# A language-model tower on one core: two biases moved from TensorE to VectorE, two buffers of transposed rows, a loop of two turns, small products ahead of the last z

## The chip, the cores and the metric

The kernel runs on one core of a Trainium2 chip. The metric is the device time of one execution in microseconds (us). The median of three runs of the kernel before is 1307.63 us (1302.93 to 1309.92). A change of this kernel under about 0.5%, 6.5 us, can't be told from none.

## What is computed

64 sequences of 128 token ids go through four stages. All is fp32 unless said.

```python
table = concat([quantize_ste(tw[i] * ts[i], [16, 8, 6, 4][i]) for i in range(4)])   # 50257 x 256
x = layernorm(take(table, ids))
# block: Mamba-like mixer, then an MLP
proj = rms(x) @ in_proj_w.T                 # z (512), u (512), B, C (16 each), dt (8 heads)
u, B, C = silu(causal depthwise conv of 4 taps + conv_b); B, C normalised; dt = softplus(dt + dt_bias)
# two-state recurrence over 128 steps for 8 heads x 64 x 16, read out with C -> ys
x = x + ((ys + D_skip * u) * silu(z)) @ out_proj_w.T + out_proj_b
x = x + gelu(rms(x) @ fc1_w.T + fc1_b) @ fc2_w.T + fc2_b
# layernorm, one absmax over everything, int8 rounding, int8-weight product, scale, bias, add x
```

The quantising of the table needs the largest magnitude of each tier, so the whole table of 51 MB is read once.

## The kernel before

**Stage 1** (0 to 175 us, lines 163 to 415). SyncE streams the table into a ring of six tiles. ScalarE takes magnitudes (L248), VectorE folds them into running maxima (L346), GpSimd gathers the token rows (L232), TensorE makes each token's tier scale (L286), and VectorE multiplies it into pairs of tokens (L337, `scale_tokens`). In the same stream VectorE scales `w_in` by the first norm's weights (L390), unpacks `w_q` (L391) and makes `ident_b` (L393). The late weights are loaded last (`LATE_WEIGHTS`, L222). A barrier ends the stage.

**Stage 2** (175 to 1250 us). 16 groups of four sequences (512 tokens) go through a software pipeline of 19 turns, written once per engine (`pe_turn`, `act_turn`, `dve_turn`, `pool_turn`) and called by `turns`. In turn g group g is in its first part (norm, transposes, u, small products B, C, dt), group p = g-1 in its second (z, scan, output product) and group m = g-2 in its third (MLP) and, with g-3, in the search for the absmax. Turns 4 to 14 are a hardware loop of one turn; the others are straight code. The order of an engine's instructions within a turn is written by hand, and semaphores join them.

TensorE's order in a turn: z of two of the four row tiles (`pe_z`), transposes of group g's rows (`pe_transpose_rows`, L631), z of the other two, transposes of the MLP's rows (`pe_mlp_T`, L1145), small products (`pe_small`, L657), eight fc1 tiles (L1172) with fc2 three behind (L1193), transposes of u (L1017), scores (L1057) and scan products (L1078) of the two head groups, u products 0, 1 and 2, 3 (`pe_u`, L646), output product (`pe_out`, L1106). A small matmul for the norms of B and C (`pe_ss`, L705) lies among fc1.

`xT`, the transposed rows, has one buffer. The z of group p reads it and so do u and the small products of group g, so ScalarE's copy into it (`act_rows_T`, L642) waits for the last z (`z_left`, `z_mm`), and the small products wait for that copy.

The two biases are added by TensorE: `pe_bias` (L567) multiplies a 0/1 matrix `pick` with the bias split in three bf16 parts, one 128x512 matmul for each of two PSUM banks. It runs twice before the output product (L1101) and twice before the first fc2 (L1190). ScalarE seeds the two fc2 banks with x (`act_seed`, L1159).

ScalarE's order from the z on: silu of z 0, 1 (L1005), the MLP's normed rows (`act_rms_rows`, L1139, which waits for L631's transposes), silu z 2, `xT`, `mT` (L1152), silu z 3, the small inputs (L667 to L670), seed, silu of B and C, exp/ln of dt, the norm's ln/exp, then eight gelus (L1182).

VectorE's order from the scores on: masks of head group 0 (`dve_mask`, L1068), `dve_h2` (fc2 plus x, L1204), skip of tiles 0, 1 (`dve_skip`, L1085), masks of head group 1, gate 0, 1 (`dve_gate`, L1092), skip 2, 3, gate 2, 3, the convolution of u (L972), x plus the output product (`dve_x2`, L1113). `pe_u` waits for the skip of the same tile, whose bank it overwrites (L950).

GpSimd runs 60 of the 64 steps of the recurrence (L796, L798) and the small powers (L603, L1130). In the last turns the maximum of the last group is taken by ScalarE (`act_x3`, L1245) and VectorE (`dve_max3`, L1251).

**Stage 3** (1250 us to the end): rounding, int8-weight product, output.

Of the kernel before, what the change touches and what calls it, by code (L numbers as in the profile page):

```python
# [31 lines left out]
I8 = mybir.dt.int8  # L32
# [55 lines left out]
def build(nc, a, out):  # L88
    with ExitStack() as ctx:
# [22 lines left out]
        bias3 = sb("bias3", [P, 2, D], BF16)  # L112
# [43 lines left out]
        LATE_WEIGHTS = ((w_fc1, "w_fc1"), (w_out, "w_out"), (w_fc2, "w_fc2"))  # L156
        OUT_B, FC2_B = 0, 1
# [5 lines left out]
        with ExitStack() as part:  # L163
# [37 lines left out]
            PAIRS = SEQS // 2  # L201
            SETS = 3
            HOT_FROM = 4
            pair_bank = (bank[0], bank[1], bank[4], bank[5], bank[6], bank[7])
# [33 lines left out]
            def _(act):  # L238
# [21 lines left out]
                for n in range(HOT_FROM + QUADS, len(tiles)):  # L260
                    magnitude(n)

# [37 lines left out]
            def _(dve):  # L300
# [30 lines left out]
                def scale_tokens(upto):  # L331

                    while scaled[0] < upto:
                        n = scaled[0]
                        dve.wait_ge(gathered[2 * n // GATHERS], 16 * GATHERS)
                        dve.wait_ge(ts_row, n + 1)
                        dve.tensor_tensor(h[:, 2 * n * D:(2 * n + 2) * D], pair_bank[n % (2 * SETS)][:, :],  # L337
                                          h[:, 2 * n * D:(2 * n + 2) * D], ALU.mult).then_inc(ts_used, 1)
                        scaled[0] += 1
# [28 lines left out]
                for n, (_, np_, nr, tier) in enumerate(tiles):  # L368
# [15 lines left out]
                    if n >= HOT_FROM + 2:  # L384
                        scale_tokens(min(PAIRS, 2 * (n - HOT_FROM - 1)))
                    if n == HOT_FROM + QUADS + 1:

                        dve.wait_ge(weight_in, 16 * len(WEIGHTS))
                        for k in range(KD):
                            dve.tensor_scalar(w_in[:, k, :], w_in[:, k, :], c("norm1", k), None, ALU.mult)  # L390
                        dve.tensor_copy(w_q[:].rearrange("p k c -> p (k c)"),  # L391
                                        w8[:].rearrange("p k c -> p (k c)").bitcast(I8))
                        dve.tensor_copy(ident_b[:], ident[:])  # L393
# [31 lines left out]
        xT = sb("xT", [P, KD, TOK])  # L425
# [38 lines left out]
        mx3 = sb("mx3", [P, G])  # L464

# [5 lines left out]
        bias_in, halved, pick_cleared = sem("bias_in"), sem("halved"), sem("pick_cleared")  # L471
# [37 lines left out]
        z_left = signal("z_left", 1)  # L509
# [19 lines left out]
        seeded = signal("seeded", 2)  # L529
        h2_ready = signal("h2_ready", 2)  # L530
# [5 lines left out]
        mx = signal("mx", 2)  # L536

# [10 lines left out]
        def dve_split_biases(dve):  # L548

            whole, rest = utok[:, 0, :], utok[:, 1, :]  # L550
            b3 = bias3[:].rearrange("p i c -> p (i c)")
# [4 lines left out]
            dve.wait_ge(bias_in, 16)  # L556
            dve.tensor_copy(b3, whole).then_inc(halved, 1)
# [9 lines left out]
        def pe_bias(pe, dst, i, start):  # L567
            pe.matmul(dst[:, :].rearrange("p (j c) -> p j c", j=2), pick[:],
                      bias3[:, i, :].unsqueeze(1).to_broadcast([P, 2, D]), start=start, stop=False,
# [64 lines left out]
        def act_rows_T(act, g):  # L634
            for k in range(KD):
                if since(g) and k == 0:

                    act.wait_ge(z_left.sem, z_left.at(g - 1))
                elif since(g):
                    act.wait_ge(z_mm.sem, z_mm.at(g - 1))  # L640
                act.wait_ge(xr_T.sem, xr_T.at(g, k + 1))
                act.activation(xT[:, k, :], tb[k][:, :], ACT.Copy).then_inc(xT_ready.sem, 1)  # L642

        def project(pe, dst, c0, c1, done):
            for k in range(KD):
                last = pe.matmul(dst, w_in[:, k, c0:c1], xT[:, k, :], start=(k == 0), stop=(k == KD - 1))  # L646
            last.then_inc(done, 1)

        def pe_small(pe, g):
# [1199 lines left out]
```

## Time and profile before

| what | us |
|---|---|
| median of three runs | 1307.63 |
| the profiled execution, its own time | 1309.22 |
| its span | 1307.3 |
| TensorE busy | 1156.5 (88%) |
| VectorE busy | 1083.3 (83%) |
| ScalarE busy | 791.4 (61%) |
| GpSimd busy | 698.2 (53%) |

Matmul ends are modelled in a trace: consecutive groups overlap a little, so the distance from start to start is what a group costs, and "busy" hides short waits. The page's chain that ended last covers only stage 3, since barriers part the stages; stages 1 and 2 are read from timelines. An fp32 matmul shows as two records. In a timeline the bracket gives the engine's idle time before the row and what ended it.

### The profile page before, as it was taken

Reading aid. Unit: us, or ns where it says so; the run is one execution under the profiler, and the core shown is the slowest. Engines: PE = TensorE matmul, PEld = TensorE weight load, DVE = VectorE, ACT = ScalarE, POOL = GpSimd, SP = SyncE. Lnnn points to the kernel's source line nnn. Section 1 sums busy time; section 2 is a strip of 40 time slices with the busy share of each in tenths; the row PEclk is TensorE's granted clock in tenths of the full one; section 3 lists DMA queues with packets and bytes.
Section 4 is the critical chain, followed back from the end, with each engine's and each line's share of the span. In section 5 each row is a group of like instructions: output and inputs, shape, how many; then the busy total and the mean of one; then the engine's idle time right before and its main releaser. Section 6 shows DMA issues by size and latency. Waiting matters only on the chain. (4 is left out here: it accounts for less than half of the span.)

```text
span 1307.3 us, 25029 instructions
## 1 busy us (share of the span) xinstructions
PE 1156.5 (88%) x7317; PEld 764.9 (59%) x7324; DVE 1083.3 (83%) x1963; ACT 791.4 (61%) x1275; POOL 698.2 (53%) x2062
## 2 busy tenths in 40 slices
PE   2991055899999999999999999999999999999956
PEld 1550022567676757676666667676767676757534
DVE  5997979978888888888888888898888887776177
ACT  4666637374848484848485756657574848452367
POOL 8882010657575857575757575757666574730000
PEclk9999997899999999999999999999999999998979
DMA  9999901010101010101010000000010101000025
GB/s 363 408 408 417 372 10 42 8 36 1 36 2 35 2 35 0 35 2 33 5 30 11 24 17 17 18 16 22 13 35 0 35 0 35 2 19 1 1 68 190
DMA packets 36993, 91.60 MB, mean 70 GB/s; under 512 B 10125, under 2 KB 21474, under 8 KB 32594
## 3 DMA queue, kind: packets, MB, share of 16 engines
q1 hardware_dynamic: 33298, 81.32, 17.9%
q0 software_dynamic: 3072, 8.39, 1.7%
q10 hardware_dynamic: 576, 1.31, 0.3%
q8 instruction: 23, 0.38, 0.1%
q14 instruction: 24, 0.20, 0.1%
HBM read 81.29 MB, written 9.70 MB: 70 GB/s over the span
## 5 line engine op out<-in xcount | busy, mean ns | idle before, releaser
L796 POOL TENSOR_TENSOR stp<-Gs,X 128x32 f32<-128x32 f32 x900 | 260.8, 290 | 254.5 <-ACT X L769 176.2
L798 POOL TENSOR_TENSOR Gs<-Gs,stp 128x32 f32<-128x32 f32 x900 | 257.9, 287 | 70.4
L1193 PE MATMUL bank<-w_fc,gl 128*128 128x256 f32 x1024 | 246.8, 385 | 0.8 <-ACT gl L1182 0.7
L1172 PE MATMUL bank<-mT,w_fc 128*128 128x512 f32 x512 | 236.7, 595 | 1.5 <-ACT mT L1152 1.5
L1193 PEld LDWEIGHTS bank<-w_fc,gl 128*128 128x128 f32 x1024 | 190.5, 191 | 59.9 <-issue 25.3
L646 PE MATMUL bank<-xT,w_in 128*128 128x512 f32 x448 | 208.7, 606 | 0.4 <-DVE uT L1085 0.3
L958 ACT ACTIVATE uT<-bank,cols 128x512 f32<-128x512 f32 x64 | 47.9, 774 | 216.6 <-DVE sz L1092 197.8
L1172 PEld LDWEIGHTS bank<-mT,w_fc 128*128 128x128 f32 x512 | 94.9, 190 | 85.5 <-issue 79.7
L972 DVE SCALAR_TENSOR_TENSOR uT<-bank,cols,uT 128x500 f32<-128x500 f32 (+1 forms) x192 | 133.4, 735 | 2.3
L646 PEld LDWEIGHTS bank<-xT,w_in 128*128 128x128 f32 x448 | 82.1, 192 | 84.7 <-issue 78.4
L346 DVE TENSOR_TENSOR peak<-ring,peak 128x1536 f32<-128x1536 f32 (+2 forms) x67 | 115.3, 1721 | 8.2 <-ACT ring L248 6.5
L248 ACT ACTIVATE ring<-ring 128x3072 f32<-128x3072 f32 (+4 forms) x36 | 90.8, 2531 | 50.5 <-DMA ring<-in_table 50.5
L1106 PE MATMUL bank<-w_out,sz 128*128 128x256 f32 x512 | 115.7, 379 | 0.0
L1068 DVE TENSOR_TENSOR MT<-bank,causal 128x512 f32<-128x512 f32 x128 | 79.4, 683 | 43.1 <-PE bank L1057 43.1
L1182 ACT ACTIVATE gl<-bank,cols 128x512 f32<-128x512 f32 x128 | 81.3, 681 | 51.5 <-PE bank L1193 48.9
L1106 PEld LDWEIGHTS bank<-w_out,sz 128*128 128x128 f32 x512 | 97.3, 190 | 19.4 <-issue 5.0
L937 DVE RECIPROCAL rm<-rm 128x512 f32<-128x512 f32 x32 | 107.1, 3348 | 0.5
L769 ACT ACTIVATE X<-d_rep,cols 128x512 f32<-128x512 f32 x64 | 72.0, 1198 | 35.2 <-DMA d_rep<-d_rows 35.2
L232 POOL DMA_INDIRECT h<-in_table,ids x64 | 82.2, 1285 | 19.4 <-issue 19.4
L286 PE MATMUL bank<-ts,hot 4*128 4x256 f32 x128 | 60.3, 648 | 20.0 <-ACT hot L259 14.6
L1078 PEld LDWEIGHTS bank<-MT,utok 128*64 128x64 f32 x1024 | 57.6, 141 | 20.6 <-issue 13.0
L1057 PE MATMUL bank<-Qf,Kf 32*128 32x64 f32 x2048 | 66.7, 279 | 2.2 <-ACT gl L1182 1.5
(211 smaller groups left out, 1879.4 us busy)
## 6 DMA issues: line engine op xcount, KB each, us to landing
ring<-in_table SPq DMA_DIRECT2D x31, 1536.0 KB, 19.9
d_rep<-d_rows SPq DMA_DIRECT2D x128, 64.0 KB, 2.0
out<-res SPq DMA_DIRECT2D x16, 512.0 KB, 2.9
b_rep<-bc_rows SPq DMA_DIRECT2D x128, 32.0 KB, 1.8
c_rep<-bc_rows SPq DMA_DIRECT2D x128, 32.0 KB, 1.8
w_fc<-in_w_fc SPq DMA_DIRECT2D x2, 1024.0 KB, 9.3
ring<-in_table SPq DMA_DIRECT2D x2, 768.0 KB, 5.3
w_in<-in_w_in ACTq DMA_DIRECT2D x1, 1088.0 KB, 5.1
```

What stands on the lines that cost most here:

```text
L232: pool.indirect_dma_start(out=h[:, b * D:(b + 1) * D], out_offset=None, in_=table, in_offset=bass.IndirectOffsetOnAxis(ap=ids[:, b:b + 1], ...
L248: act.activation(ring[n % RING][0:np_, 0:nr, :], ring[n % RING][0:np_, 0:nr, :], ACT.Abs) \
L346: return dve.tensor_tensor(acc, ring[t][0:np_, r0:r0 + nr, :], acc, ALU.max)
L646: last = pe.matmul(dst, w_in[:, k, c0:c1], xT[:, k, :], start=(k == 0), stop=(k == KD - 1))
L796: pool.tensor_tensor(stp[:], Gs[:, t, ::-1, :], X2[:, t, :, :], ALU.mult).then_inc(rec.sem, 1)
L798: pool.tensor_tensor(Gs[:, t + 1, :, :], Gs[:, t, :, :], stp[:], ALU.add).then_inc(rec.sem, 1)
L937: dve.reciprocal(half_rm, half_rm).then_inc(inverted.sem, 1)
L972: dve.scalar_tensor_tensor(acc[:, :, i:], ps[:, :, 0:LEN - i], c("u_tap", f * TAPS + TAPS - 1 - i), acc[:, :, i:], ALU.mult, ALU.add).then ...
L1106: last = pe.matmul(bank[n][:, (j % 2) * D:(j % 2 + 1) * D], sz[:, f, j * LEN:(j + 1) * LEN], w_out[:, f, :], start=False, stop=(f == UT - ...
L1172: last = pe.matmul(pj[n % 4][:, :], w_fc1[:, k, n * P:(n + 1) * P], mT[:, k, :], start=(k == 0), stop=(k == KD - 1))
L1182: act.activation(gl[n % LEAD][:], pj[n % 4][:, :], ACT.Gelu_apprx_tanh, bias=c("fc1_bias", n)) \
L1193: last = pe.matmul(sbk[j // 2][:, (j % 2) * D:(j % 2 + 1) * D], gl[n % LEAD][:, j * LEN:(j + 1) * LEN], w_fc2[:, n, :], start=False, stop= ...
```

## The change

- `pe_bias` is gone from the fc2 product; the fc2 bias is added by `dve_fc2_bias` to the rows in `h`, after gate 0, 1. The output bias is added by `dve_out_bias` to `xl`, after `dve_h2`, in turns that have a first and a third part (2 to 15); in turns 1 and 16 TensorE still adds it. Each is one VectorE instruction on 128x1024, both inputs in SBUF, the bias broadcast over four rows. `dve_x2` waits for `xl_biased`, `dve_h2` for `biased`.
- `xT` has two buffers; `act_rows_T` no longer waits for the last z. `z_left` is gone.
- TensorE: `pe_mlp_T` and `pe_small` go ahead of the last z. ScalarE: `act_rows_T`, `act_mlp_T` and `act_small_in` go ahead of silu z 2; silu z 3 goes behind `act_small_silu`; the seed goes behind `act_small_dt`.
- The loop holds two turns, 4 to 13; turns 14 and 15 are straight code.
- Stage 1: `w_in`, `w_q` and `ident_b` are made by ScalarE after its last magnitude; the last four token pairs are scaled by VectorE in stage 2, after the statistics of group 0, and TensorE waits for them. Four small memsets and two copies into `Gs` move behind the first quantising. The split of the bias is half as wide.
- SyncE: the 256 KB bias load at the start of stage 2 becomes two 128 KB loads at the end of the late weights.
- Turn 1: four warm matmuls after the first scores. Turn 16: u transposes earlier. Turn 18: eight warm matmuls. Last group's maximum: VectorE's `dve_extremes` in place of `act_x3` and `dve_max3`.

```diff
+        def dve_scale_pair(dve, n):
+            dve.wait_ge(gathered[2 * n // GATHERS], 16 * GATHERS)
+            dve.wait_ge(ts_row, n + 1)
+            dve.tensor_tensor(h[:, 2 * n * D:(2 * n + 2) * D], pair_bank[n % len(pair_bank)][:, :],
+                              h[:, 2 * n * D:(2 * n + 2) * D], ALU.mult).then_inc(ts_used, 1)
...
+                for k in range(KD):
+                    act.activation(w_in[:, k, :], w_in[:, k, :], ACT.Copy, scale=c("norm1", k))
...
-                        scale_tokens(min(PAIRS, 2 * (n - HOT_FROM - 1)))
+                        scale_tokens(min(PAIRS - HELD, 2 * (n - HOT_FROM - 1)))
...
-        xT = sb("xT", [P, KD, TOK])
+        xT = [sb(f"xT{i}", [P, KD, TOK]) for i in range(2)]
...
-                if since(g) and k == 0:
-                    act.wait_ge(z_left.sem, z_left.at(g - 1))
-                elif since(g):
-                    act.wait_ge(z_mm.sem, z_mm.at(g - 1))
...
+        def dve_out_bias(dve, g):
+            dve.wait_ge(xl_ready.sem, xl_ready.at(g))
+            dve.tensor_tensor(xl[:], xl[:], out_b[:].unsqueeze(1).to_broadcast([P, G, D]), ALU.add) \
+                .then_inc(xl_biased.sem, 1)
+        def dve_fc2_bias(dve, g):
+            dve.wait_ge(xl_ready.sem, xl_ready.at(g))
+            dve.tensor_tensor(rows(g, 0, G).rearrange("p (j c) -> p j c", j=G),
+                              rows(g, 0, G).rearrange("p (j c) -> p j c", j=G),
+                              fc2_b[:].unsqueeze(1).to_broadcast([P, G, D]), ALU.add).then_inc(biased.sem, 1)
...
-                for i in range(2):
-                    pe_bias(pe, sbk[i], FC2_B, False)
...
+        def dve_extremes(dve, g):
+            ends3 = rows(g, 0, G).rearrange("p (j c) -> p j c", j=G)
+            dve.wait_ge(h2_ready.sem, h2_ready.at(g))
+            dve.tensor_reduce(mx3[:], ends3, AX.X, ALU.max).then_inc(extreme, 1)
+            dve.tensor_reduce(mn3[:], ends3, AX.X, ALU.min).then_inc(extreme, 1)
...
+                    if f == UT - 1:
+                        if third:
+                            if not second:
+                                pe_warm(pe, pj[0], 5)
+                            pe_mlp_T(pe, m)
+                        if first:
+                            pe_small(pe, g, b)
                     if second:
-                        pe_z(pe, p, f)
-                if third:
-                    if not second:
-                        pe_warm(pe, pj[0], 5)
-                    pe_mlp_T(pe, m)
-                if first:
-                    pe_small(pe, g)
+                        pe_z(pe, p, f, 1 - b)
...
+                        if not third:
+                            pe_warm(pe, sbk[0], 4)
...
+                if not third and fourth:
+                    pe_warm(pe, pj[0], 8)
...
                 if first and third:
                     dve_h2(dve, m)
+                    dve_out_bias(dve, p)
...
                     dve_gate(dve, p, (0, 1))
+                    if first and third:
+                        dve_fc2_bias(dve, p)
                     dve_skip(dve, p, (2, 3))
```

## Rows read from the trace of the kernel before

**Rows 1.** The page, part 1: busy time and share of each engine.
```profile
PE 1156.5 (88%) x7317; PEld 764.9 (59%) x7324; DVE 1083.3 (83%) x1963; ACT 791.4 (61%) x1275; POOL 698.2 (53%) x2062
```

**Rows 2.** TensorE's timeline in one steady turn: start, length, line, operation, tiles, count.
```profile
573.13 3.70 PE L646 MATMUL bank<-xT,w_in 128*128 128x512 f32 x8
576.67 0.38 PE L568 MATMUL bank<-bias,pick 128*128 128x512 bf16 x1
576.89 3.62 PE L1106 MATMUL bank<-w_out,sz 128*128 128x256 f32 x16
...
590.03 1.88 PE L993 MATMUL bank<-xT,w_in 128*128 128x512 f32 x4
...
600.92 0.59 PE L568 MATMUL bank<-bias,pick 128*128 128x512 bf16 x2
601.41 1.99 PE L1193 MATMUL bank<-w_fc,gl 128*128 128x256 f32 x8
```

**Rows 3.** TensorE's timeline, the same products u 2, 3 in turns 1 and 15.
```profile
259.86 3.70 PE L646 MATMUL bank<-xT,w_in 128*128 128x512 f32 x8 [0.26 <-DVE uT L1085]
...
1135.96 3.70 PE L646 MATMUL bank<-xT,w_in 128*128 128x512 f32 x8
```

**Rows 4.** ScalarE's timeline in the steady turn.
```profile
588.52 1.71 ACT L1139 ACTIVATE xr<-xl,ssq 128x256 f32<-128x256 f32 x4 [0.28 <-PE bank L631]
...
600.66 1.84 ACT L1182 ACTIVATE gl<-bank,cols 128x512 f32<-128x512 f32 x3
```

**Rows 5.** VectorE's timeline in the steady turn.
```profile
567.69 2.48 DVE L1068 TENSOR_TENSOR MT<-bank,causal 128x512 f32<-128x512 f32 x4 [0.68 <-PE bank L1057]
570.10 1.44 DVE L1092 TENSOR_TENSOR sz<-sz,uT 128x512 f32<-128x512 f32 x2
572.33 1.62 DVE L1085 SCALAR_TENSOR_TENSOR uT<-uT,cols,bank 128x512 f32<-128x512 f32 x2 [0.80 <-PE bank L1078]
```

**Rows 6.** Groups by line, 500 to 900 us: busy us, mean ns, then idle before.
```profile
L943 DVE SCALAR_TENSOR_TENSOR Qf<-rm,Qf 128x512 f32<-128x512 f32 x12 | 12.4, 1037 | 0.4
...
L931 DVE TENSOR_TENSOR rm<-utok 128x1024 f32<-128x1024 f32 x6 | 7.4, 1225 | 0.2
```

**Rows 7.** VectorE's timeline in turn 0: a 1024-wide operation and the next start.
```profile
205.05 1.22 DVE L824 TENSOR_TENSOR utok<-X 128x1024 f32<-128x1024 f32 x1
206.19 0.42 DVE L826 TENSOR_SCALAR utok<-utok 128x512 f32<-128x512 f32 x1
```

**Rows 8.** GpSimd's timeline in the steady turn.
```profile
570.08 0.25 POOL L798 TENSOR_TENSOR Gs<-Gs,stp 128x32 f32<-128x32 f32 x1
570.41 0.58 POOL L796 TENSOR_TENSOR stp<-Gs,X 128x32 f32<-128x32 f32 x1
...
585.99 0.21 POOL L1128 TENSOR_TENSOR ssq<-ssq,eps 128x4 f32<-128x4 f32 x1 [2.17 <-ACT gl L1122]
```

**Rows 9.** VectorE's timeline at the end of stage 1.
```profile
113.99 1.29 DVE L337 TENSOR_TENSOR h<-bank,h 128x512 f32<-128x512 f32 x2 [3.62 <-DMA h<-in_table,ids]
...
119.97 1.47 DVE L390 TENSOR_SCALAR w_in<-w_in,cols 128x1088 f32<-128x1088 f32 x2
...
121.83 46.58 DVE L346 TENSOR_TENSOR peak<-ring,peak 128x1536 f32<-128x1536 f32 x26
```

**Rows 10.** ScalarE's timeline, the last magnitudes of stage 1.
```profile
152.00 5.51 ACT L248 ACTIVATE ring<-ring 128x3072 f32<-128x3072 f32 x3 [0.95 <-DMA ring<-in_table]
```

**Rows 11.** TensorE's timeline in turns 1, 16 and 17.
```profile
245.67 3.68 PE L1078 MATMUL bank<-MT,utok 128*64 128x128 f32 x32 [3.32 <-DVE MT L1068]
...
1182.39 2.65 PE L1057 MATMUL bank<-Qf,Kf 32*128 32x64 f32 x64 [1.50 <-ACT gl L1182]
...
1234.56 7.07 PE L1193 MATMUL bank<-w_fc,gl 128*128 128x256 f32 x32
```

**Rows 12.** Stretches: length, busy by engine, granted TensorE clock, DMA share, GB/s.
```profile
246.00:252.00 6.00, 6.00 (x84) 5.67 (x80) 4.71 (x12) 0.00 (x0) 4.59 (x19) 0.50 0.01 3
...
1183.00:1189.00 6.00, 6.00 (x64) 4.69 (x61) 3.41 (x5) 0.47 (x1) 0.00 (x0) 0.55 0.01 3
```

**Rows 13.** VectorE's timeline in turns 1 and 18.
```profile
253.04 2.48 DVE L1068 TENSOR_TENSOR MT<-bank,causal 128x512 f32<-128x512 f32 x4 [2.33 <-PE bank L1057]
...
1248.47 1.22 DVE L1251 TENSOR_REDUCE mx<-rm 128x4 f32<-128x1024 f32 x1 [3.94 <-ACT rm L1245]
```

More of the change, by code:

```diff
@@ L1276, in pe_turn, with turn @@
         def pe_turn(pe):
-            def turn(g, first, second, third, fourth, nxt):
+            def turn(g, b, first, second, third, fourth, nxt):
                 p, m = g - 1, g - 2
@@ L1330, in turn @@
                 if first:
-                    pe_u(pe, g, (2, 3))
+                    pe_u(pe, g, (2, 3), b)
                 if second:
-                    pe_out(pe, p, sbk if first else tb)
+                    pe_out(pe, p, sbk if first else tb, not (first and third))
+                if not third and fourth:
+                    pe_warm(pe, pj[0], 8)
             turns(pe, turn)
         def act_turn(act):
-            def turn(g, first, second, third, fourth, nxt):
+            def turn(g, b, first, second, third, fourth, nxt):
                 p, m = g - 1, g - 2
@@ L1369, in turn @@
                         act_u_tap0(act, g, (2, 3))
-                if fourth and not second:
+                if fourth and third and not second:
                     act_x3(act, g - 3, GROUPS - 1)
@@ L1403, in dve_turn, with turn @@
         def dve_turn(dve):
-            def turn(g, first, second, third, fourth, nxt):
+            def turn(g, b, first, second, third, fourth, nxt):
                 p, m = g - 1, g - 2
@@ L1447, in turn @@
                     dve_h2(dve, m)
-                if fourth and not second:
+                    dve_out_bias(dve, p)
+                if fourth and third and not second:
                     dve_max3(dve, g - 3)
@@ L1458, in turn @@
                     dve_gate(dve, p, (0, 1))
+                    if first and third:
+                        dve_fc2_bias(dve, p)
                     dve_skip(dve, p, (2, 3))
                     dve_gate(dve, p, (2, 3))
+                if second and not first:
+                    dve_fc2_bias(dve, p)
                 if second and not first:
@@ L1466, in turn @@
                 if second:
-                    dve_x2(dve, p, 0, sbk if first else tb)
+                    dve_x2(dve, p, 0, sbk if first else tb, first and third)
                 if first and second:
@@ L1470, in turn @@
                 if second:
-                    dve_x2(dve, p, 1, sbk if first else tb)
+                    dve_x2(dve, p, 1, sbk if first else tb, first and third)
                 if first and second:
                     dve_bc(dve, g)
+                if filling:
+                    dve_fc2_bias(dve, p)
                 if fourth and second:
@@ L1479, in turn @@
                     dve_mean3(dve, m)
+                    if not second:
+                        dve_extremes(dve, m)
             dve_quantise(dve, 0)
+            dve.memset(eps5[:], 1e-5)
+            dve.memset(eps6[:], 1e-6)
+            dve.memset(minus[:], -1.0)
+            dve.memset(half[:], -0.5).then_inc(begun, 1)
             dve_row_stats(dve, 0)
+            for n in range(PAIRS - HELD, PAIRS):
+                dve_scale_pair(dve, n)
+            dve.tensor_copy(Gs[:, 0, 0, :], c("part0").to_broadcast([P, LANES]))
+            dve.tensor_copy(Gs[:, 0, 1, :], c("part1").to_broadcast([P, LANES]))
             turns(dve, turn)
         def pool_turn(pool):
-            def turn(g, first, second, third, fourth, nxt):
+            def turn(g, b, first, second, third, fourth, nxt):
                 p, m = g - 1, g - 2
@@ L1504, in _, with turn @@
             def _(sp):
-                sp.dma_start(utok[:, 0, :], a["bias"]).then_inc(bias_in, 16)
-                def turn(g, first, second, third, fourth, nxt):
+                def turn(g, b, first, second, third, fourth, nxt):
                     if first:
```

173 lines of the change are left out of this document (91 added, 82 removed).

## The prediction

> **What bounds the kernel now.** I read the page's busy shares first [rows 1], then TensorE's timeline of one steady turn [rows 2], then the timelines of the engines that feed it. The reader is to see three things. First, TensorE has hardly a hole in stage 2: in [rows 2] each group starts where the one before ends, and from the u 2, 3 products of turn 1 to those of turn 15 [rows 3] there are 14 turns in 1135.96 - 259.86 = 876.10 us, 62.58 us each. Second, it is bound by itself but only just. VectorE sits idle for 0.68 us before the second masks and for 0.80 us before skip 2 [rows 5], and u 2, 3 start at 573.13, right as skip 2 is done (572.33 + half of 1.62 = 573.14). The first fc2 starts at 601.41, right after the first gelu (600.66 plus a third of 1.84, with a row's fill: 601.3) [rows 2, 4]. Third, stage 1 ends late on VectorE: its folds run without a hole from 121.83 to 168.4 [rows 9], while the last magnitudes are done at 152.00 + 5.51 = 157.5 [rows 10].
>
> **The steady turn.** I measure it from the start U of u 2, 3 (573.13) to the next U.
>
> - Output bias off TensorE: 576.89 - 576.67 = 0.22 us, twice: -0.44.
> - fc2 bias off TensorE: two matmuls between 600.92 and 601.41 [rows 2]. They fill time in which TensorE would wait for the first gelu anyway. Worth at most 0.49; by itself I take 0.
> - New order. ScalarE's normed rows can't start before the transposes L631 and end at 588.52 + 1.71 = 590.23 [rows 4]. TensorE, with z 2 done, would be free for `pe_mlp_T` at 590.03 [rows 2], where z 3 covered this before. So it now waits about 0.3 us. The later copies into `xT` and `mT` then run on ScalarE (4 copies, some 0.54 each) beside the transposes, small products and z 3, and cost TensorE nothing more. Bounds: 0.1 and 0.8.
> - ScalarE's chain to the first gelu. In before it runs without a gap. The small inputs now come before silu z 2, but silu of B and C waits for VectorE's small convolution, and VectorE is not free for it earlier than before. Adding the same instructions in the new order I come to the first fc2 at U + 28.05, against 601.41 - 573.13 = 28.28: -0.25. That is what the 0.44 less 0.3 and the reordering leave; the rest is wait.
> - Two additions on VectorE between scores and u 2, 3. The nearest operation is L931, 1225 ns for 128x1024 with both inputs in SBUF [rows 6]; the next instruction starts 1.14 us after such a one [rows 7]. Against 2 x 1.15 stand the idle 0.68 and 0.80 us [rows 5] and two overlaps of 0.08: 2.30 - 1.64 = +0.66. Gates beside GpSimd take 1.44 rather than 1.28 for two, so an addition may take 0.05 more; a shorter semaphore wait may give as much. I take +0.60. Queued behind the additions are skip 2 and 3, and TensorE's u 2 waits for them.
>
> Sum: -0.25 + 0.60 = +0.35 a turn, times 14 = **+4.9 us**. Bounds of a turn: if neither the additions nor the wait bites, all four bias matmuls go, 4 x 0.22 = -0.9. If the additions take their full 1.23 and nothing is won at the gelu, 2.46 - 1.48 = +1.0.
>
> Edits with no price: the second `xT` buffer only lifts a wait; loops of two turns save branches that TensorE's queue hides (its groups abut at the turn's end); `dve_x2`'s and `dve_h2`'s new waits are on instructions long done. The DMAs: SyncE issues two 128 KB loads more behind the late weights and none in stage 2. They land before the barrier, which comes some 10 us after the last ring tile; if not, they would cost about their transfer, 0.7 us at the stage's 400 GB/s.
>
> **GpSimd.** Beside two gates (570.10 to 571.54) its step takes 0.58 instead of 0.25 us [rows 5, 8], so additions of this kind hold it up, some 1.2 us each at most. It has an idle of 2.17 us before L1128 in every turn [rows 8], and the recurrence can start about 1 us earlier since the small inputs come earlier. So 2.4 us are covered: 0. The Trainium skill, "SBUF — State Buffer", section "SBUF: two separate sides", says that a VectorE operation with two SBUF inputs and a GpSimd operation exclude each other for the whole instruction; by that rule each addition stops GpSimd for its full length, which is the 1.2 us that the row bounds. The row agrees with the direction of the rule.
>
> **Stage 1.** Off VectorE go the scale of `w_in` and the two casts (121.83 - 119.97 = 1.86 us), four pairs of tokens (2 x 1.29), and the wait of 3.62 us for the last gather that the first of those pairs ended [rows 9]: 8.1 us. VectorE then follows ScalarE's magnitudes, which come 3.7 us apart while two folds take 3.58. From the last magnitude's end at 157.5 [rows 10] and the backlog of one and a half tiles, I get folds done at 162.0 in place of 168.4: **-6.4**. ScalarE's new work (two scales of 1.15 and two casts) runs from 157.5 to 161 beside this. The pairs come back in stage 2: 2.5 us on VectorE after the statistics of group 0, beside GpSimd's powers, ScalarE's norm and TensorE's warm matmuls, with about 1 us to spare before the small convolution of turn 0; cost 0, and 2.5 without that cover. Bounds: 0 (transfers set the stage's end) and -8.1.
>
> **Turn 1.** TensorE idles 3.32 us and then works at half the clock (granted 0.50, that is 1.2 GHz, from 246 to 252) [rows 11, 12], so that VectorE waits 2.33 us for the second scores [rows 13]. Four warm matmuls of 0.86 fill the hole; the two groups that took 3.6 each take 1.94. VectorE then is the bound, so no more than its 2.33 is won; a hole of some 1.8 us comes before u 2, 3. I take **-2.0**, bounds 0 and -2.3. The Trainium skill, "TensorE: Matmul & The Clock Gate", section "Loop structure matters more than you think", holds that dense work keeps the clock and a long wait drops it; by it the sum is the same -2.0, or nothing if the hole before u 2, 3 drops the clock again.
>
> **The last turns.** Turn 16: mlp_T ahead of z 3 and no fc2 bias bring the first fc2 about 1.0 earlier; earlier u transposes bring another 0.7 before the scores at 1182.39, whose wait was 1.50 [rows 11]. Its stretch at half clock (0.55) [rows 12] may shrink: **-2.0**, bounds -1 and -4.9. Turn 17: two bias matmuls, **-0.4**. Turn 18: VectorE waited 3.94 us for ScalarE's rows before the last maximum at 1248.47, which ended at 1249.9 [rows 13]; the new seven instructions would end at 1247.8. But eight warm matmuls of 0.86 begin at 1234.56 + 7.07 = 1241.6 [rows 11] and end at 1248.5, ahead of the barrier: -1.3, and 0.3 for a stage 3 that starts at full clock: **-1.6**.
>
> **Sum.** 4.9 - 6.4 - 2.0 - 2.0 - 0.4 - 1.6 = -7.5. The profiled execution took 1309.22, which gives 1301.7; the median is 1.59 lower, so 1300.1 for a median.
>
> **Rivals.**
>
> 1. *TensorE stays the bound.* The additions fit in VectorE's idle time (masks could start sooner than I think) and the turn gets 0.4 shorter. For it: VectorE has 1.48 us idle just there [rows 5]. Against: 2.3 us of work. 14 x -0.4 - 12.4 = -18.0: 1289.6.
> 2. *The edges give little.* Stage 1 is set by the transfers or by something behind the barrier, and only 1.0 of the 6.4 arrives. For it: magnitudes wait for a DMA before every tile [rows 10]. Against: VectorE's backlog of 11 us at the end. -7.5 + 5.4 = -2.1: 1305.5.
> 3. *Slower: the additions are dear.* Place: between the gate and skip 2. Price: a VectorE operation of strided form takes 1037 ns for 512 elements (L943) [rows 6]; if the broadcast or the lock with GpSimd makes an addition 2.07, the turn grows by 2 x 2.07 - 1.64 - 0.25 = +2.25, 14 x 2.25 - 12.4 = +19: 1326.7. It decides from (6.5 + 12.4) / 14 = 1.35 us a turn, an addition of 1.6 us. Against: the mask also broadcasts an input and takes the plain 2.48 us for four [rows 5].
>
> **Chances.** My forecast 0.45, with its own range of 1296 to 1305; rival 1 0.25; rival 2 0.20; rival 3 0.10. Faster by over 0.5% (below 1301.1): 0.6 of my case, 0.27, and rival 1: 0.52. Same: the rest of my case and rival 2: 0.38. Slower: 0.10. The range holds my case, rival 2 and nearly all of rival 1: 1289 to 1308.
>
> **What would show it.** In the profile after, the fold group ends at 162 and stage 2 starts near 169.3. From the u 2, 3 of turn 1 to that of turn 15 it is 14 x 62.9 = 881 us; a value under 876 speaks for rival 1, over 890 for rival 3. VectorE shows no idle before skip 2, and u 2 waits for it. L1145 waits some 0.3 us for L1139, and the first fc2 for the first gelu. GpSimd's idle before L1128 shrinks but stays. The scan products of turn 1 run at full clock, and the last maximum no longer waits for ScalarE. The prediction is wrong if the turn gets shorter, or if the barrier of stage 1 stays near 175.

## The result, and the profile after

The changed kernel takes 1312.63 us (median of 9 runs, 1311.28 to 1314.27), the kernel before 1307.44 in the same session: ratio 1.0043, with a 95% interval of 1.0031 to 1.0055. That is a loss of 0.4%: under the 0.5% set above, though the interval excludes none, and 12.5 us above the forecast of 1300.1. The three groups of experiments below ran in other sessions, in which the kernel before took 1306.1 to 1307.4 us, so medians of different groups are comparable to about 1.3 us only. The profiled executions stand 1311.28 to 1309.22, so a sum made against the traces has to come to +2.1.

The page of the kernel after, its busy shares [rows 1] and, from part 3, the queues that load instructions (packets, MB, share of 16 engines):

```profile
span 1309.4 us, 24524 instructions
...
PE 1158.1 (88%) x7281; PEld 761.3 (58%) x7288; DVE 1112.9 (85%) x1994; ACT 792.4 (61%) x1275; POOL 721.8 (55%) x2062
...
q8 instruction: 66, 1.08, 0.4%
...
q14 instruction: 77, 0.63, 0.2%
```

The same two lines of the page before are:

```profile
q8 instruction: 23, 0.38, 0.1%
q14 instruction: 24, 0.20, 0.1%
```

VectorE works 30 us more, TensorE 2. The new thing is that three times as much code is loaded: a program's instructions reach the engines by DMA too, and q8 and q14 are the queues that carry them.

TensorE's timeline after, the products u 2, 3 in turns 1, 6, 7, 8 and 15 [rows 3]:

```profile
249.86 1.55 PE L650 MATMUL bank<-xT,w_in 128*128 128x512 f32 x3 [1.74 <-DVE uT L1092]
...
567.35 1.12 PE L650 MATMUL bank<-xT,w_in 128*128 128x512 f32 x2 [0.45 <-DVE uT L1092]
...
629.67 1.55 PE L650 MATMUL bank<-xT,w_in 128*128 128x512 f32 x3 [0.46 <-DVE uT L1092]
...
696.77 1.55 PE L650 MATMUL bank<-xT,w_in 128*128 128x512 f32 x3 [0.44 <-DVE uT L1092]
...
1142.87 1.55 PE L650 MATMUL bank<-xT,w_in 128*128 128x512 f32 x3 [0.46 <-DVE uT L1092]
```

Turn 1 is 10 us early, turn 15 is 6.91 us late. In between the turns are not alike: 629.67 - 567.35 = 62.32, but 696.77 - 629.67 = 67.10. All 14 intervals, read from the starts of this group, are 63.40, 62.53, 62.42, 62.32, **66.82**, 62.32, **67.10**, 62.32, **66.88**, 62.33, **67.19**, 62.32, 62.53, 62.53. The four long ones lie where the engines jump back to the start of the loop's body, which holds two turns and runs five times. In the trace before all steady turns take 62.46.

The long turn on three engines. VectorE's timeline, the last instructions of one pass of the body and the first of the next:

```profile
645.75 0.27 DVE L1232 COPY mu<-mv 128x4 f32 x1
649.01 1.44 DVE L583 TENSOR_SCALAR h<-h,tok  x4 [3.00 <-issue]
...
652.16 1.11 DVE L704 SCALAR_TENSOR_TENSOR bc<-bank,cols,bc 128x127 f32<-128x127 f32 x3
```

ScalarE's timeline in the same stretch:

```profile
653.31 0.31 ACT L685 ACTIVATE bc<-bc 128x128 f32<-128x128 f32 x1 [2.99 <-DVE bc L704]
...
659.69 1.84 ACT L1194 ACTIVATE gl<-bank,cols 128x512 f32<-128x512 f32 x3
```

TensorE's timeline there:

```profile
654.34 3.60 PE L1184 MATMUL bank<-mT,w_fc 128*128 128x512 f32 x8
660.43 3.68 PE L1203 MATMUL bank<-w_fc,gl 128*128 128x256 f32 x8 [2.50 <-ACT gl L1194]
```

And the two stretches around that wait (length, busy by engine, granted clock, DMA share, GB/s):

```profile
655.00:660.00 5.00, 2.93 (x7) 0.95 (x5) 3.50 (x12) 4.86 (x10) 1.86 (x4) 1.00 0.03 5
660.00:665.00 5.00, 4.57 (x11) 3.43 (x12) 4.79 (x14) 3.34 (x4) 0.00 (x0) 0.66 0.38 107
```

Read from the top: VectorE stands 3.00 us for nothing that the trace shows ("issue") before its first quantise. The small convolution L704 is queued behind it, so ScalarE waits 2.99 us for it, the first gelu is late, and TensorE waits 2.50 us at the first fc2. After that wait the granted clock is 0.66 for the next 5 us (part of them at 1.2 GHz), and eight fc2 matmuls that take 1.99 in an undisturbed turn take 3.68 (3.03 to 3.68 at the four jumps). Kernel before, VectorE's timeline at the same place, with a body of one turn:

```profile
590.32 1.38 DVE L576 TENSOR_SCALAR h<-h,tok  x4 [0.46 <-issue]
```

The whole of it as a ledger, from the profiled executions (us):

| stretch | before | after | difference | predicted |
|---|---|---|---|---|
| start to VectorE's first instruction of stage 2 | 175.82 | 168.45 | -7.37 | -6.4 |
| to u 2, 3 of turn 1 | 84.04 | 81.41 | -2.63 | -2.0 |
| 14 turns, without the excess of the four long ones | 876.10 | 874.30 | -1.80 | +4.9 |
| excess of four long turns over 62.32 | 0 | 18.71 | +18.71 | 0 |
| u 2, 3 of turn 15 to the last fc2 group (L1193, L1203) | 98.60 | 94.90 | -3.70 | -2.4 |
| to the first maximum of stage 3 | 15.64 | 14.23 | -1.41 | -1.6 |
| to the end of the span | 57.1 | 57.4 | +0.3 | 0 |

The sum is +2.1. Everything but one row came to -16.6, and that row took 18.7 back.

### The profile page after: what moved, and what is told of

Same layout as the page of the kernel before. It is cut to its first block and busy times, and to the rows that moved or that the text cites. A ratio compares the mean times of both kernels' runs of the same rounds, so it can differ in the third digit from the quotient of the medians.

```text
span 1309.4 us, 24524 instructions
## 1 busy us (share of the span) xinstructions
PE 1158.1 (88%) x7281; PEld 761.3 (58%) x7288; DVE 1112.9 (85%) x1994; ACT 792.4 (61%) x1275; POOL 721.8 (55%) x2062
## 5 line engine op out<-in xcount | busy, mean ns | idle before, releaser
L800 POOL TENSOR_TENSOR stp<-Gs,X 128x32 f32<-128x32 f32 x900 | 274.6, 305 | 254.9 <-ACT X L773 127.6
L802 POOL TENSOR_TENSOR Gs<-Gs,stp 128x32 f32<-128x32 f32 x900 | 264.1, 293 | 70.8
L1203 PE MATMUL bank<-w_fc,gl 128*128 128x256 f32 x1024 | 251.6, 390 | 10.0 <-ACT gl L1194 10.0
L650 PE MATMUL bank<-xT,w_in 128*128 128x512 f32 x512 | 239.5, 606 | 8.8 <-DVE uT L1092 8.5
L1203 PEld LDWEIGHTS bank<-w_fc,gl 128*128 128x128 f32 x1024 | 194.1, 194 | 74.3 <-issue 32.0
L650 PEld LDWEIGHTS bank<-xT,w_in 128*128 128x128 f32 x512 | 92.2, 191 | 104.7 <-issue 89.8
L773 ACT ACTIVATE X<-d_rep,cols 128x512 f32<-128x512 f32 x64 | 72.1, 1199 | 26.3 <-DMA d_rep<-d_rows 26.3
L1064 PEld LDWEIGHTS bank<-Qf,Kf 32*128 32x128 f32 x2048 | 60.1, 186 | 10.3 <-issue 10.3
```

Of the source, the lines that this page charges most:

```text
L650: last = pe.matmul(dst, w_in[:, k, c0:c1], x[:, k, :], start=(k == 0), stop=(k == KD - 1))
L800: pool.tensor_tensor(stp[:], Gs[:, t, ::-1, :], X2[:, t, :, :], ALU.mult).then_inc(rec.sem, 1)
L802: pool.tensor_tensor(Gs[:, t + 1, :, :], Gs[:, t, :, :], stp[:], ALU.add).then_inc(rec.sem, 1)
L1064: last = pe.matmul(score_bank[hh][:, t:t + CL], Kf[own, hg * G + j, ch * CL:ch * CL + P], Qf[own, hg, t:t + CL], start=True, stop=True)
L1203: last = pe.matmul(sbk[j // 2][:, (j % 2) * D:(j % 2 + 1) * D], gl[n % LEAD][:, j * LEN:(j + 1) * LEN], w_fc2[:, n, :], start=False, stop= ...
```

## The experiments

Ratios are to the kernel before, run beside each on the same chip (medians 1307.38, 1306.05 and 1306.12 for the three groups). "VectorE one" means that VectorE's loop holds one turn.

| kernel | median us | ratio, 95% interval |
|---|---|---|
| after, VectorE one (a_dve1) | 1295.51 | 0.9910, 0.9894 to 0.9927 |
| after, one turn on VectorE, GpSimd, SyncE (a_dps1) | 1296.21 | 0.9921, 0.9902 to 0.9941 |
| after, no loop on any engine (a_flat) | 1295.78 | 0.9905, 0.9885 to 0.9924 |
| before, VectorE two (b_dve2) | 1310.98 | 1.0029, 1.0016 to 1.0042 |
| after, old order (a_late) | 1307.86 | 1.0013, 1.0001 to 1.0024 |
| VectorE one, old order (a_dve1late) | 1300.93 | 0.9957, 0.9943 to 0.9970 |
| VectorE one, output bias on TensorE (a_outpe) | 1297.26 | 0.9930, 0.9908 to 0.9951 |
| VectorE one, fc2 bias early (a_fc2early) | 1291.33 | 0.9886, 0.9867 to 0.9905 |
| before with the new stage 1 (b_stage1) | 1300.73 | 0.9950, 0.9931 to 0.9970 |
| fc2 bias early, no warm matmuls in turn 1 (fe_nowarm1) | 1291.70 | 0.9892, 0.9865 to 0.9919 |
| fc2 bias early, none in turn 18 (fe_nowarm18) | 1290.16 | 0.9871, 0.9845 to 0.9897 |
| fc2 bias early, neither (fe_nowarm) | 1289.70 | 0.9870, 0.9843 to 0.9897 |

### The loop of two turns

**a_dve1**: the loop of one turn is given back to VectorE alone.

```diff
-            with eng.Fori(2, GROUPS // 2 - 1) as i:
-                turn(i * 2, 0, True, True, True, True, True)
-                turn(i * 2 + 1, 1, True, True, True, True, True)
-            turn(GROUPS - 2, 0, True, True, True, True, True)
+            if single:
+                with eng.Fori(4, GROUPS - 1) as g:
+                    turn(g, 0, True, True, True, True, True)
+            else:
+                with eng.Fori(2, GROUPS // 2 - 1) as i:
...
-            turns(dve, turn)
+            turns(dve, turn, True)
```

> The changed kernel, but VectorE's loop of stage 2 holds one turn again (turns 4 to 14), all other engines keep the loop of two. Theory (fetch): in the changed kernel the turn behind each of the 4 back edges is 4.5 to 4.9 us longer than the rest, since VectorE's first quantise (L583) waits 3.0 us for nothing that the trace shows, while its body of two turns is loaded again. With a body of one turn this wait goes: 4 x 4.6 = 18.4 us less, 1294 us, and no turn from turn 4 on above 62.6 us. Rival 1 (other engines' back edges cost as much): the long turns stay, 1309 to 1313 us. Rival 2 (the additions on VectorE are what the turn pays for): all turns stay as they are, 1312 us.

1295.51: 17.1 us off the changed kernel. The 14 turns take 876.25 us and none of those in the loop is above 62.7. VectorE's timeline behind a jump:

```profile
643.28 1.38 DVE L583 TENSOR_SCALAR h<-h,tok  x4 [0.41 <-issue]
```

**a_dps1**: the same on GpSimd and SyncE too (`turns(pool, turn, True)`, `turns(sp, turn, True)`).

> The changed kernel, with loops of one turn on VectorE, GpSimd and SyncE; TensorE and ScalarE keep the loop of two turns. Theory (fetch on VectorE alone): as with VectorE's loop alone, about 1294 us. Rival 1 (GpSimd's or SyncE's back edge counts too): 1 to 4 us below the kernel with VectorE's loop alone. Rival 2 (TensorE's or ScalarE's back edge is what costs): the long turns stay, 1309 to 1313 us.

1296.21, no different. The instruction queues on the page of a_dve1:

```profile
q8 instruction: 66, 1.08, 0.3%
q14 instruction: 54, 0.44, 0.1%
```

And on this kernel's page, where q8 is the same:

```profile
q14 instruction: 26, 0.21, 0.1%
```

GpSimd or SyncE had loaded 28 packets again and again as well, and it cost nothing here. So on q14 it is not that code is loaded, but who waits for it. The 66 packets on q8, against 23 before, are the same in all three kernels, so they aren't VectorE's, GpSimd's or SyncE's; by elimination they belong to TensorE or ScalarE. What they cost isn't shown: no run of the changed kernel takes the loop of two turns from those engines without writing the turns out.

**a_flat**: turns 4 to 14 written out on all engines.

```diff
-            with eng.Fori(2, GROUPS // 2 - 1) as i:
-                turn(i * 2, 0, True, True, True, True, True)
-                turn(i * 2 + 1, 1, True, True, True, True, True)
-            turn(GROUPS - 2, 0, True, True, True, True, True)
+            for g in range(4, GROUPS - 1):
+                turn(g, g % 2, True, True, True, True, True)
```

> The changed kernel with turns 4 to 14 as straight code on every engine, no loop. Theory (a back edge out of a long body costs, straight code doesn't): no long turns, 1294 us, the same as with VectorE's loop of one turn within 2 us. Rival 1 (it is the amount of code read, not the jump): code is then read in all 11 turns, some 15 us or more slower than with VectorE's loop of one turn. Rival 2 (the additions are the cost): 1312 us.

1295.78. Its instruction queues:

```profile
q8 instruction: 56, 0.92, 0.3%
q14 instruction: 53, 0.43, 0.1%
```

Nearly as much code is loaded as in a_dve1 on q14 (54 packets), all turns from turn 4 on take 62.5 to 62.7, and VectorE has no wait before L583 at all. The rival that the amount of code on q14 counts is out: straight code is loaded beside the work, while a jump back out of a long body is waited for. The DMA records bear this out: in after, b_dve2 and a_late a packet of q14 starts 0.8 to 1.1 us into each of the twelve long waits. The Trainium skill says this of an engine's code, "Runtime: NRT & Kernel Launch", section "Instruction fetch mechanics": it is prefetched in sequence, and a taken branch to a page that isn't held stalls the engine until the page is fetched. The traces agree with it; that the code behind the jump was no longer held is inferred from these packets, and the 3.0 us is the trace's.

**b_dve2**: the kernel before, VectorE's loop alone two turns long.

```diff
+            if double:
+                with eng.Fori(2, GROUPS // 2 - 1) as i:
+                    turn(i * 2, True, True, True, True, True)
+                    turn(i * 2 + 1, True, True, True, True, True)
+                turn(GROUPS - 2, True, True, True, True, True)
```

> The kernel before the change, with only VectorE's loop made two turns long. Nothing is computed otherwise. Theory (fetch): the turn behind each of 4 back edges gets 3 to 4.6 us longer, 12 to 18 us in all: 1320 to 1326 us. Rival 1 (the loss needs the changed kernel's order of work, for instance the small convolution ahead of the last z): within 3 us of the kernel before, 1307 us. Rival 2 (other engines' back edges): 1307 us as well, and the kernel with VectorE's loop of one turn tells them apart.

1310.98, +3.6: more than nothing, but far under the 12 expected and close to rival 1 (within 3 us), which had the order of work decide. The stall is there in full. The first quantise (L576) in this kernel's view by source line, 430 to 1000 us, with what its engine waited for (us, times):

```profile
L576 DVE TENSOR_SCALAR h<-h,tok x36: 404/410/469, 463.3 to 967.7; - x36
its engine sat idle before it (us, times) until:
  issue: 12.4, 4
```

VectorE's timeline behind one of the jumps:

```profile
654.63 1.38 DVE L576 TENSOR_SCALAR h<-h,tok  x4 [3.12 <-issue]
```

The instruction queue that grew, on the page of this kernel:

```profile
q14 instruction: 47, 0.39, 0.1%
```

TensorE's timeline at the first fc2 behind that jump:

```profile
663.98 1.99 PE L1193 MATMUL bank<-w_fc,gl 128*128 128x256 f32 x8 [0.56 <-ACT gl L1182]
```

12.4 us in 4 waits, 3.1 each, and 23 packets more on q14 than before (24), the same 23 that a_dve1 saves against after. But only 0.9 us of each reaches TensorE (turns of 63.37 among 62.47), whose wait of 0.56 leaves its clock alone. So the stall has one length and, by the kernel, different prices.

### What the price of the stall hangs on

**a_late**: the changed kernel, loops of two turns, old order of work.

```diff
                 for f in range(UT):
                     if first and f == 2:
                         pe_transpose_rows(pe, g)
-                    if f == UT - 1:
-                        if third:
-                            if not second:
-                                pe_warm(pe, pj[0], 5)
-                            pe_mlp_T(pe, m)
-                        if first:
-                            pe_small(pe, g, b)
                     if second:
                         pe_z(pe, p, f, 1 - b)
+                if third:
+                    if not second:
+                        pe_warm(pe, pj[0], 5)
+                    pe_mlp_T(pe, m)
+                if first:
+                    pe_small(pe, g, b)
```

(ScalarE's order is turned back in the same way.)

> The changed kernel with its loops of two turns, but the transposed MLP rows and the small products behind the last z again, on TensorE and ScalarE (both transposed-row buffers and the biases on VectorE stay). What is asked: how much of the 3.0 us that VectorE stands at each of 4 back edges reaches TensorE. Theory (the order decides the price of the stall): with z 3 between the transposes and the small products VectorE has more slack before its small convolution, so that about 0.9 us a back edge arrives, as in the kernel before with VectorE's loop of two turns, and not 4.6: some 15 us less than the changed kernel, 1296 to 1300 us. Rival (the additions and the stall together make the price, not the order): the long turns stay near 66.9 us and the time near 1312 us.

1307.86: 4.8 us less than after (3.9 by the ratios), where some 15 were expected, and so in the range of neither theory nor rival. VectorE still stands 3.14 us, by its timeline behind a jump:

```profile
650.93 1.38 DVE L583 TENSOR_SCALAR h<-h,tok  x4 [3.14 <-issue]
```

TensorE's timeline then shows a wait of 0.98 for the gelu and a clock that is kept:

```profile
660.58 1.99 PE L1203 MATMUL bank<-w_fc,gl 128*128 128x256 f32 x8 [0.98 <-ACT gl L1194]
```

The turns behind a jump take 64.2 to 64.6, but the others grew too, to 63.1 to 63.4. What the old order costs without any stall was missing from my expectation, so it was measured by itself.

**a_dve1late**: the same edit on a_dve1.

> The changed kernel with VectorE's loop of one turn, and the transposed MLP rows and small products behind the last z again on TensorE and ScalarE. With no stall at the back edge left, this shows what the new order itself is worth. Theory: in the steady turn hardly anything (62.5 to 62.6 us, since TensorE is busy in both), about 1 us in turn 16, where the mlp rows come earlier: 1296 to 1297 us. Rival (the new order carries the gain of the steady turn): the turn grows by 0.5 us and more, 1302 us.

1300.93, so the rival had it: beside loops of two turns on the other engines the new order is worth 5.4 us (6.1 by the ratios). With the runs so far, medians in us:

| | loops of two | VectorE one | the stalls cost |
|---|---|---|---|
| new order | 1312.63 | 1295.51 | 17.1 |
| old order | 1307.86 | 1300.93 | 6.9 |

TensorE's waits before its fc2 matmuls (L1203) and ScalarE's before the time-step factors (L773), 300 to 1130 us (us, times), in a_dve1late:

```profile
  ACT gl L1194: 27.3, 41
...
  DMA d_rep<-d_rows: 32.4, 13
```

The same two in a_dve1:

```profile
  ACT gl L1194: 10.3, 24
...
  DMA d_rep<-d_rows: 20.2, 13
```

The new order starts the small inputs earlier, the DMA that replicates the time steps lands about 0.9 us earlier for ScalarE (32.4 against 20.2 in 13 turns), and the gelus, some of which are queued behind that wait, hold TensorE 17 us less in sum; 5.6 of it shows in the 14 turns (881.81 and 876.25). Which link of that chain brings how much was not taken apart: in the kernel before ScalarE waits 28.5 us in 13 turns at that DMA too, and TensorE only 11.7 at fc2.

The traces show one link more. Of the 5.6 us, 4.3 lie in the five turns 5, 7, 9, 11 and 13, the second ones of the loop's body (63.1 to 63.5 us each, against 62.6 to 62.9 for the first ones). SyncE's timeline of a_dve1late, the eight issues of that DMA in turns 5 and 6:

```profile
468.19 4.63 SPq L745 DMA_DIRECT2D d_rep<-d_rows  x8
...
532.04 3.68 SPq L745 DMA_DIRECT2D d_rep<-d_rows  x8
```

ScalarE's timeline, the instruction that waits for it in the same turns:

```profile
474.55 4.49 ACT L773 ACTIVATE X<-d_rep,cols 128x512 f32<-128x512 f32 x4 [3.19 <-DMA d_rep<-d_rows]
...
537.29 4.52 ACT L773 ACTIVATE X<-d_rep,cols 128x512 f32<-128x512 f32 x4 [2.11 <-DMA d_rep<-d_rows]
```

In each of the five turns one of the eight issues takes 1.2 to 1.5 us where the others take some 0.4, and a packet of q8 starts within 0.2 us of its start. The kernel before has neither such a packet nor such an issue from 450 to 1100 us (3.55 us for eight), and its turns there are all alike. In a_dve1 the slow issues are there too, but no turn is longer for them. So much of what the new order wins may be shelter from the code that the long body of another engine loads, and not a gain over the order of the kernel before; the old order with both additions and loops of one turn on all engines was not run.

The new order also puts the small convolution where VectorE has no slack for a stall. With the stall it loses 4.8, without it it wins 5.4.

### The biases

**a_outpe**: `pe_out(..., True)` in all turns, `dve_out_bias` dropped, on a_dve1.

> The changed kernel with VectorE's loop of one turn, and the output bias back on TensorE in all turns; the fc2 bias stays on VectorE. An addition of about 1.13 us leaves VectorE between the scores and u 2, 3, and two matmuls of 0.22 us come back. Theory (VectorE bounds that stretch): scores to u 2, 3 falls by about 0.5 (13.86 to 13.3), the matmuls give 0.44 back: 1295 us within 2 us, so this half of the change is worth nothing by itself. Rival 1 (TensorE alone sets the turn): 0.44 us a turn more, 1300 us. Rival 2 (the addition costs its whole length): 0.7 us a turn less, 1288 us.

1297.26; the 14 turns take 876.31 us against 876.25. In the turns the theory holds: scores to u 2, 3 takes 13.50 in place of 13.86, and u 2, 3 to the first fc2 28.10 in place of 27.68. So the turn agrees with the theory, while the median lies just outside its 1293 to 1297; the difference of medians, 1.8, isn't in the turns, and where it arises stays open.

**a_fc2early**: the fc2 bias ahead of the first masks, on a_dve1.

```diff
+                if first and third:
+                    dve_fc2_bias(dve, p)
                 if second:
                     for hh in range(4):
                         dve_mask(dve, p, 0, hh)
...
                     dve_gate(dve, p, (0, 1))
-                    if first and third:
-                        dve_fc2_bias(dve, p)
                     dve_skip(dve, p, (2, 3))
```

> The changed kernel with VectorE's loop of one turn, and in the steady turn the fc2 bias is added ahead of the first masks, where VectorE idles 1.33 us for the scores, and not between the first gates and skip 2. Theory (VectorE sets the start of u 2, 3, so that an addition there costs its 1.13 us less the idle time it eats): from the scores to u 2, 3 it takes 13.3 us in place of 13.86, a turn of 62.0 in place of 62.5, 11 x 0.5 us in the steady turns: 1290 us (1288 to 1292). Rival (another engine takes over, or u 2, 3 wait for the scores on another way): 1294 to 1296 us.

1291.33, inside the expected 1288 to 1292; the 14 turns take 871.29 us, 0.35 less each, where 0.5 was expected: scores to u 2, 3 takes 13.3 us in some turns and up to 13.8 in others. VectorE's timeline: it now has a hole before skip 2 again, as in [rows 5].

```profile
559.50 1.34 DVE L1099 TENSOR_TENSOR sz<-sz,uT 128x512 f32<-128x512 f32 x2
561.35 1.62 DVE L1092 SCALAR_TENSOR_TENSOR uT<-uT,cols,bank 128x512 f32<-128x512 f32 x2 [0.52 <-PE bank L1085]
```

### Stage 1 and the warm matmuls

**b_stage1**: the change's stage 1 alone on the kernel before (the scales and casts on ScalarE, the last four pairs of tokens behind the first statistics of stage 2).

> The kernel before with the change's stage 1 alone: scale of the input weights and both casts on ScalarE, four pairs of tokens scaled in stage 2. Theory (VectorE's folds set the end of stage 1): the folds end near 161 instead of 168.4 and stage 2 starts 7.4 us earlier, 1300 us (1299 to 1301). Rival (part of it is given back in turn 0, where VectorE has the pairs to scale): 1302 to 1304 us.

1300.73, 5.3 us less, with an interval of 3.9 to 9.0. In its trace stage 2 starts at 168.44, the 7.4 us in full, and the span is 8.7 shorter than that of before. How much of the 7.4 a median keeps stays open: the profiled execution before was 1.8 us above its median.

**fe_nowarm1, fe_nowarm18, fe_nowarm**: a_fc2early without one or both of

```diff
-                        if not third:
-                            pe_warm(pe, sbk[0], 4)
...
-                if not third and fourth:
-                    pe_warm(pe, pj[0], 8)
```

> The kernel with VectorE's loop of one turn and the early fc2 bias, without the four warm matmuls of turn 1. Theory of the prediction (they keep TensorE's clock up for the scan products, 2.0 us): these take 3.4 to 3.7 us again instead of 2.1, and the time is 1293 us, 2 us more. Rival (turn 1 is VectorE's, and the kernel before with the new stage 1 alone reached u 2, 3 of turn 1 at 250.90 with cold products, against 250.47 with warm ones): 0 to 0.5 us more, 1291 to 1292 us.

> The kernel with VectorE's loop of one turn and the early fc2 bias, without the eight warm matmuls of turn 18. Theory: they end 0.9 us after the last maximum, so stage 3 waits for them, and the clock falls to 0.50 in the first microseconds of stage 3 in spite of them. Without them stage 3 starts 0.9 us earlier: 1290.5 us. Rival (as predicted, they give stage 3 a faster start): 0.3 us more or the same, 1291.5 us.

> The kernel with VectorE's loop of one turn and the early fc2 bias, without either group of warm matmuls of the change. If both are as the rivals of the single runs have it, 1290.5 to 1291.5 us; if both do what they are there for, 1293.5 us.

1291.70, 1290.16 and 1289.70 against 1291.33: none is told from the others by its interval. The traces say more. Turn 1 of fe_nowarm1, TensorE:

```profile
238.70 3.51 PE L1085 MATMUL bank<-MT,utok 128*64 128x128 f32 x32 [3.31 <-DVE MT L1075]
...
251.01 2.41 PE L650 MATMUL bank<-xT,w_in 128*128 128x512 f32 x5 [1.33 <-DVE uT L1092]
```

The products are cold again (3.51 for 2.14), yet u 2, 3 start at 251.01 against 250.47 with warm ones: 0.5 us, not 2.0. In both TensorE waits for VectorE there (1.33 and 1.74 us), so VectorE sets that start. The other pair, fe_nowarm and fe_nowarm18, gives 1.0 (253.46 and 252.46); there the scores before run at the lower clock in both. The end of turn 18 on TensorE, first in a_fc2early:

```profile
1221.93 7.03 PE L1307 MATMUL bank<-w_out,ident 128*128 128x512 f32 x16
1229.47 0.27 PE L1656 MATMUL bank<-ident,xmax 128*1 128x128 f32 x1 [0.51 <-DVE xmax L1771]
```

The same in fe_nowarm18, with the last fc2 group:

```profile
1219.43 7.07 PE L1203 MATMUL bank<-w_fc,gl 128*128 128x256 f32 x32
1233.04 0.37 PE L1654 MATMUL bank<-ident,xmax 128*1 128x128 f32 x1 [6.54 <-DVE xmax L1769]
```

From the last fc2 group to the first matmul of stage 3 it is 13.61 us without the eight warm ones and 14.45 (1229.47 - 1215.02) with them: they end at 1228.96, 0.9 us behind the last maximum (1228.1), and all engines wait for them. Both lengths are the same to 0.01 us in every trace of a kernel without and with them, so this 0.8 is shown. From there to the end it takes 58.1 without and 57.7 with; but this last part takes anything from 55.9 to 58.2 in the traces that have the warm matmuls, and 57.7 in that of fe_nowarm. So whether the 0.8 reaches the end can't be told.

## Why the prediction was wrong

The step that failed is this sentence among the edits with no price: "loops of two turns save branches that TensorE's queue hides". It looked at TensorE's jump alone. The loop is built once and run by every engine, and on VectorE a body of two turns makes each of the four jumps 2.9 to 3.2 us long, instead of 0.40 to 0.56 for a body of one. Priced at 0, it measured 18.7 us in the trace and 17.1 in the medians. Nothing in the trace before shows a long body, so it had to be a term with bounds, and a rival of its own: the slower rival that I gave, dear additions, was the wrong one. Put right, the forecast would have read "-7.5 if the body is still held", and that is the sign of a_dve1.

**The steady turn.** Predicted +0.35 (62.81 for the 62.46 of a turn in the loop before), measured 62.32 between jumps and 62.50 in a_dve1: -0.14 and +0.04. Without the jumps the turn got shorter, which the prediction itself named as a sign of being wrong. The two additions were about right: 1.22 and 1.27 us, the next start 1.13 and 1.19 later, scores to u 2, 3 13.77 for 13.28, +0.49 against +0.60. VectorE has no hole before skip 2 and u 2, 3 wait 0.45 for it, as said. The mis-sized term is the stretch up to the first fc2, -0.25 predicted: it is 27.65 for 28.27, -0.62. The wait of `pe_mlp_T`, where 0.3 was taken, is under 0.1 (z 2 ends at 646.60, L1157 starts at 646.68), and the time-step chain was left out. The old order with both additions costs 881.81 us for 14 turns, the new one 876.25, so beside loops of two turns the order is worth 0.40 a turn, where I had it at a fraction of 0.25; most of that lies in every second turn, as said under a_dve1late.

**GpSimd** was right: its idle time before the norm step shrinks from 2.17 us [rows 8] to 0.7 and stays; in the turn after each long one it is 3.49.

```profile
642.09 0.22 POOL L1140 TENSOR_TENSOR ssq<-ssq,eps 128x4 f32<-128x4 f32 x1 [0.68 <-ACT gl L1134]
```

**Stage 1**: -7.4 for -6.4. VectorE's folds end at 161.0 rather than at 162.0; the mechanism held.

```profile
153.90 7.13 DVE L359 TENSOR_TENSOR peak<-ring,peak 128x1536 f32<-128x1536 f32 x4 [0.17 <-ACT ring L258]
161.07 0.96 DVE L365 TENSOR_TENSOR peak<-peak 128x768 f32<-128x768 f32 x1
```

**Turn 1**: -2.6 for -2.0, but not for the reason given. The warm matmuls do keep the clock (2.1 us for the products) and bring 0.5 us by fe_nowarm1, 1.0 by the other pair. In b_stage1, which has none, turn 1 lies 9.0 us early, 1.6 more than its stage 1 explains. The rest of the 2.6 stays open: in some of the traces the scores before these products run at the lower clock (3.0 to 3.1 us in a_flat and a_outpe, 2.0 in a_dve1), and u 2, 3 come 2.3 to 2.4 us later there. That difference between executions is as large as the term.

**The last turns**: -3.7 for -2.4, and -1.4 for -1.6. In the first, turn 16 gives 3.3 for 2.0. Its scores start 1.7 us earlier, as predicted, and wait as before (1.52 us for 1.50); the rest is the clock, which was put too small: the scores and the scan products behind it run in 2.01 and 1.97 us for 2.65 and 2.79. Turn 17 gives its 0.4. In the second, the wait for ScalarE's rows is gone as predicted, but the warm matmuls don't end ahead of the barrier, and the clock is 0.50 in stage 3's first microseconds with them too (stretches of a_dve1):

```profile
1238.00:1241.00 3.00, 1.03 (x8) 0.77 (x8) 3.00 (x11) 1.11 (x3) 0.00 (x0) 0.50 0.00 0
```

**The range** of 1289 to 1308 ended under the result: its bounds were those of costs that I had named, and the one that decided had no bounds.

## What to carry to other kernels

A loop's body has a size on every engine that runs it. Before making it longer, look at each engine's share of it, and at what is queued behind the first instruction after the jump; if the loop is wanted for a buffer index, give the long body only to the engines that need the index (here TensorE and ScalarE; what the long body costs there was not measured), or write the turns out. In a profile, compare the turns with each other: a loss that sits in every second turn belongs to the loop, not to the turn's work, and the count of instruction packets confirms it. An operation added to a bound engine costs least in front of a wait that it already has: moving one addition there gave 4.2 us by the medians, 3.1 by the ratios.

## What the runs showed that I had not expected

- A jump back costs VectorE 0.40 to 0.56 us with a body of one turn and 2.9 to 3.2 with one of two, the latter in three kernels with different orders. Where between the two sizes it begins was not tried.
- The same 3.1 us cost 0.9 us a jump in b_dve2 and 4.7 in the changed kernel. 1.6 of the 4.7 comes after the wait itself, mostly from the fall of TensorE's clock behind an idle time of 2.50 us; idle times of 0.56 and 0.98 us left the clock alone.
- Loading code beside the work may not be free. On q14 it cost nothing that can be measured (a_dps1). Where a packet of q8 falls on SyncE's issues for the time steps, one of them takes 1.2 to 1.5 us instead of 0.4: no turn of a_dve1 is longer for it, but every second turn of a_dve1late is longer by 0.5 to 0.9 us. a_flat and a_dve1 differ by 0.3 us, but load nearly the same (56 and 66 packets on q8), so they don't test it. That the packet delays the issue is read from their coinciding, and no run changes it alone.
- Of the 12 kernels the best, fe_nowarm, stands at 0.9870 of the kernel before (0.9843 to 0.9897), 1289.70 us. It is the changed kernel with VectorE's loop of one turn, the fc2 bias early and without the added warm matmuls.
